# A gated delta-rule layer between two spline FFNs: two float16 halves with block scales instead of two float32r halves

## The reference

```python
qkvz = (x @ W_qkvz).reshape(b_, s_, NK, 2 * DK + 2 * R * DV)      # 16 heads of q, k; 32 of v, z; width 128
q, k, v, z = jnp.split(qkvz, [DK, 2 * DK, 2 * DK + R * DV], axis=-1)
ba = (x @ W_ba).reshape(b_, s_, NK, 2 * R)                          # beta and decay gates
# q, k, v: causal depthwise convolution of 4 taps, then silu; rms norm of q and k
def step(Sst, inp):
    q_t, k_t, v_t, g_t, beta_t = inp
    Sst = Sst * jnp.exp(g_t)[..., None, None]
    kv = jnp.einsum('bhk,bhkv->bhv', k_t, Sst)
    delta = (v_t - kv) * beta_t[..., None]
    Sst = Sst + k_t[..., None] * delta[:, :, None, :]
    o = jnp.einsum('bhk,bhkv->bhv', q_t, Sst)
    return (Sst, o)
# rms norm of o, times norm_w and silu(z), then @ W_out (4096 x 512), summed over the heads
```

## Time and profile before

| what | value |
|---|---|
| median of three runs | 3679.64 us |
| the profiled execution: span, first to last instruction | 3681.2 us |
| mean granted TensorE clock | 0.981 of 2.4 GHz |
| TensorE, matmuls | 3506.3 us busy, 95% |
| VectorE (DVE) | 2098.5 us, 57% |
| ScalarE (ACT) | 2087.1 us, 57% |
| GpSimd (POOL) | 2236.9 us, 61% |
| DMA | 268 MB moved, mean 73 GB/s |

### The profile page before, as it was taken

How to read it: one execution, slowest core, us unless ns; L and a number is a source line. 1 busy time by engine, 2 the same in 40 slices (tenths; PEclk the granted TensorE clock), 3 DMA queues, 4 the chain that set the end, 5 groups by cost and what they waited for, 6 DMA issues and landing times. The chain is left out here.

```text
span 3681.2 us, 77106 instructions
## 1 busy us (share of the span) xinstructions
PE 3506.3 (95%) x29092; PEld 2930.4 (80%) x29092; DVE 2098.5 (57%) x4063; ACT 2087.1 (57%) x5699; POOL 2236.9 (61%) x2675
## 2 busy tenths in 40 slices
PE   5997799999999999999999999999999999995998
PEld 3885588888888888888888888888888888884787
DVE  4654555555555555555555555555555555552564
ACT  3433566666666666666666666666666666662343
POOL 2112677777777777777777777777777777762110
PEclk8998899999999999999999999999999999997999
DMA  3415122222222221222222222222222122211421
GB/s 147 137 47 81 37 70 71 70 71 70 71 70 71 70 71 70 71 70 71 70 71 70 71 70 71 70 71 70 71 70 71 70 71 70 70 59 61 142 58 35
DMA packets 206383, 268.05 MB, mean 73 GB/s; under 512 B 86080, under 2 KB 116800, under 8 KB 204864
## 3 DMA queue, kind: packets, MB, share of 16 engines
q1 hardware_dynamic: 196752, 247.21, 20.5%
q0 software_dynamic: 4464, 14.36, 1.0%
q10 hardware_dynamic: 4800, 1.56, 0.3%
HBM read 173.76 MB, written 89.13 MB: 71 GB/s over the span
## 5 line engine op out<-in xcount | busy, mean ns | idle before, releaser
L1977 ACT ACTIVATE at_t<-at_inv 128x512 f16<-128x512 f32 x768 | 460.2, 599 | 472.2 <-PE at_inv L1785 472.1
L2164 DVE TENSOR_TENSOR at_pml<-at_prod,at_cst 128x256 f16<-128x256 f32 x768 | 322.7, 420 | 215.8 <-PE at_prod L1559 198.7
L1559 PE MATMUL at_proj<-x_hi,at_w_hi 128*128 128x512 f32 x1024 | 436.4, 426 | 2.7 <-PEq L1148 2.7
L1559 PE MATMUL at_proj<-x_hi,at_w_lo 128*128 128x512 f32 x1024 | 420.4, 411 | 0.0
L1559 PE MATMUL at_proj<-x_lo,at_w_hi 128*128 128x512 f32 x1024 | 415.1, 405 | 0.0
L2312 POOL TENSOR_TENSOR at_gt_lo<-at_cst,at_gates 128x512 fp32r<-128x512 f32 x256 | 261.8, 1044 | 249.6 <-PE at_misc L1559 249.6
L1559 PE MATMUL at_proj<-at_w_lo,x_hi 128*128 128x256 f32 x1024 | 314.3, 307 | 0.0
L1559 PE MATMUL at_proj<-at_w_hi,x_hi 128*128 128x256 f32 x1024 | 309.5, 302 | 0.8 <-DVE at_cv_q L2087 0.8
L1783 PEld LDWEIGHTS at_inv<-at_pml,at_t 128*128 128x128 f16 x3072 | 207.0, 97 | 120.1 <-issue 86.9
L2087 DVE SCALAR_TENSOR_TENSOR at_cv_v<-at_proj,at_cw,at_cv_v 128x511 f32<-128x511 f32 (+2 forms) x384 | 287.5, 749 | 21.8 <-ACT at_cv_v L1901 8.3
L1559 PE MATMUL at_proj<-at_w_hi,x_lo 128*128 128x256 f32 x1024 | 298.5, 292 | 0.0
(11 more groups left out here) (293 smaller groups left out, 10638.7 us busy)
## 6 DMA issues: line engine op xcount, KB each, us to landing
rows<-x SPq DMA_DIRECT2D x64, 1024.0 KB, 5.6
x<-rows SPq DMA_DIRECT2D x64, 1024.0 KB, 4.2
at_gb<-decays SPq DMA_DIRECT2D x64, 512.0 KB, 3.6
at_raw<-w_qkvz SPq DMA_DIRECT2D x45, 512.0 KB, 3.6
ffn_weights<-ffn_w SPq DMA_DIRECT2D x1, 11776.0 KB, 36.7
ffn_w<-ffn_weights POOLq DMA_DIRECT2D x4, 2688.0 KB, 23.8
at_raw<-w_out SPq DMA_DIRECT2D x16, 512.0 KB, 3.5
f_xnext<-x_in SPq DMA_DIRECT2D x4, 1024.0 KB, 5.1
```

What stands on the lines that cost most here:

```text
L1559: return nc.tensor.matmul(out, lhsT, rhs, start=start, stop=stop)
L1977: own["a_t"].up(A(grown(t16[:, s % R].rearrange("p a t -> p (a t)"), s // R), grown(psT[s % R], s // R), ACT.Copy))
L2164: own["d_p"].up(V.tensor_tensor(pml[:, level - 1, g].rearrange("p (c b a m) -> p c b a m", c=CH, a=2, m=m)[:, :, :, 0, :], psP[:, 0:S // 2 ...
```

## The change

All large operands become float16 instead of float32r, still high and low: `x_hi`, `x_lo`, `w_hi`, `w_lo`, `wo_hi`, `wo_lo`, `gt_hi`, `gt_lo`, `ba_hi`, `ba_lo`. To keep them in float16's range, x is scaled by 2^11 (in the layer norm's factor), and each block of weights (k and q, v, z, output, gates) by a power of two from its largest element, which is found on the chip: DVE reduces the raw weights along each partition, SP stores the 128 x 4 maxima to DRAM and loads them back into all partitions, DVE reduces again, keeps the exponent bits and makes a table `tab` of scales and inverse scales. POOL multiplies the raw weights by the scale before it splits them. The inverse scales go into the convolution taps (`cw`), ACT's tanh of z, and the add of the output product. norm_w leaves the gated output's copy and goes into the output weights.

The raw weights get buffers of their own (`raw_w` for three parts, `raw_o`), so that SP loads all of the next head pair's in the first unit; `gm` gets memory of its own and `mask_g(0)` and `low` lose their waits. In the norm phase the gate weights are scaled and split at chunk 7 instead of 3, and POOL's split of the first head pair's weights stands behind the scales, which DVE makes among the gates.

```diff
+def power_of_two(V, chain, mp, spread, mask, n):
+    chain(V.tensor_reduce(mp[:, 0:n], spread[:, :, 0:n].rearrange("p q n -> p n q"), mybir.AxisListType.X, ALU.max, apply_absolute_value=True))
+    chain(V.tensor_scalar(mp[:, 0:n], mp[:, 0:n], TINY, None, ALU.max))
+    chain(V.tensor_tensor(mp[:, 0:n].bitcast(I32), mp[:, 0:n].bitcast(I32), mask[:, 0:n], ALU.bitwise_and))
+
+def head_scales(V, chain, tab, mp, rcp, factors):
+    chain(V.reciprocal(rcp[:], mp[:]))
+    V.tensor_tensor(tab[:, 0:4], rcp[:], factors[:, 0:4], ALU.mult)
+    chain(V.tensor_tensor(tab[:, 4:8], mp[:], factors[:, 4:8], ALU.mult))
+    return V.tensor_tensor(tab[:, 7:8], tab[:, 7:8], mp[:, 2:3], ALU.mult)
...
@@ norm_phase, POOL @@
                     if c == 3:
-                        pool.wait_ge(consts_in, 64)
+                        pool.wait_ge(small_in, 32)
+                        nc.gpsimd.tensor_scalar(factors[:, 3:4], nw[:], 2.0 ** W_EXP, None, ALU.mult).then_inc(factors_set, 1)
+                    if c == 7:
+                        pool.wait_ge(ba_scaled, 1)
+                        nc.gpsimd.tensor_scalar(w_ba[:], w_ba[:], ba_tab[:, 0:1], None, ALU.mult).then_inc(split, 1)
...
+                pool.wait_ge(head_scaled, 1)
                 for i in range(3):
                     at = slice(i * PART, (i + 1) * PART)
-                    pool.wait_ge(raw_in[i], 16)
-                    nc.gpsimd.tensor_copy(w_hi[:, :, at], raws[i][:]).then_inc(w_split, 1)
+                    nc.gpsimd.tensor_scalar(raw_w[:, i], raw_w[:, i], tab[:, 0, i:i + 1], None, ALU.mult).then_inc(w_split, 1)
...
@@ norm_phase, DVE @@
                 for c in range(NCH - 3, NCH):
                     low(c)
+                    dve.wait_ge(raw_in[c - NCH + 3], 16)
+                    nc.vector.tensor_reduce(most[:, c - NCH + 3:c - NCH + 4], raw_w[:, c - NCH + 3].rearrange("p j n -> p (j n)"),
+                                            mybir.AxisListType.X, ALU.max, apply_absolute_value=True).then_inc(head_max, 1)
...
+                    if i == 0:
+                        dve.wait_ge(head_back, 16)
+                        dve.wait_ge(factors_set, 2)
+                        power_of_two(nc.vector, chain, mp, spread, exponent, 4)
+                        head_scales(nc.vector, chain, tab[:, 0, :], mp, rcp, factors).then_inc(head_scaled, 1)
...
@@ attn_phase, SP @@
                 if kh + 1 < NK:
+                    if kh > 0:
+                        sp.wait_ge(sems["p_w"], 2 * kh)
+                        sp.wait_ge(sems["p_z"], kh)
+                    load_part(sp, kh + 1, 0, "l_kq")
+                    load_part(sp, kh + 1, 1, "l_v")
+                    load_part(sp, kh + 1, 2, "l_z")
                     sp.wait_ge(sems["p_wo"], R * (kh + 1))
-                    load_part(sp, kh + 1, 0, "l_kq", raw_w)
+                    sp.dma_start(raw_o[:], w_out[(kh + 1) * (R * D):(kh + 2) * (R * D), :].rearrange("(r p) n -> p r n", p=P)).then_inc(sems["l_wo"], 16)
                 load_decays(first + 2)
                 next_rows(first + 1)
+                if kh + 1 < NK:
+                    sp.wait_ge(sems["d_max"], 4 * (kh + 1))
+                    sp.dma_start(most_dram, most[:]).then_inc(most_stored, 16)
+                    sp.wait_ge(most_stored, 16 * (kh + 1))
+                    sp.dma_start(spread[:].rearrange("p q n -> p (q n)"), most_dram.rearrange("q n -> (q n)").partition_broadcast(P)).then_inc(sems["l_most"], 16)
                 load_decays(first + 3)
...
@@ attn_phase, ACT @@
-                    own["a_thz"].up(A(th[:, u % 2, :], unit_bank[u][:], ACT.Tanh, scale=0.5))
+                    own["a_thz"].up(A(th[:, u % 2, :], unit_bank[u][:], ACT.Tanh, scale=tab[:, kh % 2, 6:7]))
...
-                    own["a_gt"].up(A(gt_hi[:, h, :], out_bank[:], ACT.Copy, scale=nw[:, 0:1]))
+                    own["a_gt"].up(A(gt_hi[:, h, :], out_bank[:], ACT.Copy, scale=2.0 ** GATED_EXP))
...
@@ attn_phase, DVE @@
-                    wait(dve, "s_dg", R * j if has_prep else R * (j - 1))
-                    own["d_lo"].up(V.scalar_tensor_tensor(gt_lo[:, h, :], out_bank[:], nw[:, 0:1], gt_hi[:, h, :], ALU.mult, ALU.subtract))
+                    own["d_lo"].up(V.scalar_tensor_tensor(gt_lo[:, h, :], out_bank[:], 2.0 ** GATED_EXP, gt_hi[:, h, :], ALU.mult, ALU.subtract))
...
-                    own["d_y"].up(V.tensor_tensor(row, out_bank[:], row, ALU.add))
+                    own["d_y"].up(V.scalar_tensor_tensor(row, out_bank[:], tab[:, of // B % 2, 7:8], row, ALU.mult, ALU.add))
+
+                def largest(i):
+                    new = j // B + 1
+                    wait(dve, ("l_kq", "l_v", "l_z", "l_wo")[i], 16 * (new + 1))
+                    if i < 3:
+                        own["d_max"].up(V.tensor_reduce(most[:, i:i + 1], raw_w[:, i].rearrange("p j n -> p (j n)"), mybir.AxisListType.X, ALU.max,
+                                                        apply_absolute_value=True))
+                    else:
...
+                if has_delta and j // B + 1 < NK:
+                    if j % B == 1:
+                        for i, s in enumerate((4, 9, 10, 13)):
+                            steps[s].append(lambda i=i: largest(i))
+                    if j % B == 2:
+                        steps[4].append(next_scales)
...
@@ attn_phase, POOL @@
+                wait(pool, "d_tab", kh + 1)
...
                     if hbs[0] == 0:
-                        G.tensor_copy(cw[kh % 2][:, 2 * part:2 * part + 2, :], cw_raw[:, 2 * part:2 * part + 2, :])
+                        G.tensor_scalar(cw[kh % 2][:, 2 * part:2 * part + 2, :], cw_raw[:, 2 * part:2 * part + 2, :], tab[:, kh % 2, 4 + part:5 + part], None, ALU.mult)
...
-                chain(G.tensor_copy(w_hi[:, part_rows, at], raw_w[:, part_rows]))
-                ins = G.tensor_tensor(w_lo[:, part_rows, at], raw_w[:, part_rows], w_hi[:, part_rows, at], ALU.subtract)
+                raw = raw_w[:, part, part_rows]
+                chain(G.tensor_scalar(raw, raw, tab[:, kh % 2, part:part + 1], None, ALU.mult))
+                chain(G.tensor_copy(w_hi[:, part_rows, at], raw))
+                ins = G.tensor_tensor(w_lo[:, part_rows, at], raw, w_hi[:, part_rows, at], ALU.subtract)
...
+                chain(G.tensor_scalar(raw_o[:, h], raw_o[:, h], tab[:, kh % 2, 3:4], None, ALU.mult))
+                chain(G.tensor_copy(wo_hi[:, h], raw_o[:, h]))
+                own["p_wo"].up(G.tensor_tensor(wo_lo[:, h], raw_o[:, h], wo_hi[:, h], ALU.subtract))
...
-                    wait(pool, "s_w", WPROD * j)
                     mask_g(0)
```

More of the change, by code:

```diff
@@ L1118, in norm_phase @@
         expo = sb("expo", [P, NK, NCH, R])
-        raws = [sb(f"raw{i}", [P, HB, HEADCOL // 3]) for i in range(3)]
         turn = [ctx.enter_context(nc.psum_tensor(f"nm_turn{i}", [P, 512], F32)) for i in range(3)]
@@ L1249, in copy_ba_T @@
                         act.wait_ge(ba_done, b - 1)
-                    nc.scalar.activation(ba_T[:, b % 2, :], ba_T_ps[b % 2][0:2 * NV, :], ACT.Copy).then_inc(baT_copied, 1)
+                    nc.scalar.activation(ba_T[:, b % 2, :], ba_T_ps[b % 2][0:2 * NV, :], ACT.Copy,
+                                         scale=ba_tab[0:2 * NV, 1:2]).then_inc(baT_copied, 1)
                 def scale(c):
@@ L1308, in gates_of @@
                     if b == 0:
-                        pe.wait_ge(split, 2)
+                        pe.wait_ge(split, 3)
                     if b >= 2:
@@ L2131, in out_add, with next_scales @@
                     row = rows[of % 2][:, c, :]
-                    own["d_y"].up(V.tensor_tensor(row, out_bank[:], row, ALU.add))
+                    own["d_y"].up(V.scalar_tensor_tensor(row, out_bank[:], tab[:, of // B % 2, 7:8], row, ALU.mult, ALU.add))
[4 more added lines that the diff above has]
+                        own["d_max"].up(V.tensor_reduce(most[:, i:i + 1], raw_w[:, i].rearrange("p j n -> p (j n)"), mybir.AxisListType.X, ALU.max,
+                                                        apply_absolute_value=True))
+                    else:
+                        chain(V.tensor_reduce(most[:, 3:4], raw_o[:].rearrange("p r n -> p (r n)"), mybir.AxisListType.X, ALU.max,
+                                              apply_absolute_value=True))
+                        own["d_max"].up(V.tensor_scalar(most[:, 3:4], most[:, 3:4], nw[:, 0:1], None, ALU.mult))
+                def next_scales():
+                    new = j // B + 1
+                    wait(dve, "l_most", 16 * (new + 1))
+                    power_of_two(V, chain, mp, spread, exponent, 4)
+                    own["d_tab"].up(head_scales(V, chain, tab[:, new % 2, :], mp, rcp, factors))
                 steps = {s: [] for s in range(STEPS)}
@@ L2382, in _ @@
                         sp.sem_clear(sems[n])
-                for one in spent[1::2] + [pml_set, out_done]:
+                for one in spent[1::2] + [pml_set, out_done, most_stored]:
                     sp.sem_clear(one)
@@ L2494 @@
```

(3 more changed lines are left out.)

139 lines of the change are left out of this document (86 added, 53 removed).

## The result

| | us |
|---|---|
| before, median of four runs beside the runs of after | 3678.2 |
| after, median of four runs (3830.7 to 3836.6) | 3831.4 |
| ratio, 95% interval | 1.0422 [1.0407, 1.0437] |
| forecast | 3682 (3635 to 3735) |
| profiled execution, span: before, after | 3681.2, 3830.2 |

What follows compares the result with a forecast made beforehand. The prediction took PE (TensorE) to lead, with POOL's and DVE's chains setting some pieces of each unit. 3681.2 - 90 + 86 + 7 - 1 = 3683.2 us for the span, so 3682 us for the median; range 3635 to 3735.

Steps and rivals of the forecast that it cites:

- POOL, multiplying raw weights in place: Scaling before POOL's split in the attention phase: 1.1 us for 1024 columns, 0.64 for 512; upper end 2.4 and 1.28.
- piece A: From a unit's last read-out (s_o) to turn_gated(0): POOL's 5.8 us chain sets it, half precision gains 0.
- second rival: POOL pays the two-input price for its multiplications: 4.5 us a head pair, +68, 3750 us; chance 0.15.
- Half precision, -90: Float16 matmuls in the repeated units: 0.216 us per 512-column step, -1.42 us a unit, times 63.
- rival 4: Float16 doesn't stream faster than float32r on PE: +41, 3723 us; chance 0.03.
- E: Residual and Newton with eight V matmuls on PE, until turn_kn: -0.31 us a unit.
- F: Recurrence with 24 projection matmuls in its gaps before s_o: -0.35 us a unit.
- A to D: Unit's pieces from s_o through the output products to steps 11 to 13: 0, -0.30, -0.41 and -0.05 us.
- next_scales, 2.85: DVE's table making in the third unit's fourth step, held off by POOL's instructions: 2.85 us, 0.43 without that rule.
- Rival 1: The lock doesn't hold for operations on four elements: 36 us less, 3646 us; chance 0.20.
- Norm phase, +7: DRAM round trips, reductions and POOL's later splitting before the units: +7 us, half of a 0 to 13 range.
- Rival 3: PE's new waits, above all in the third unit, let its clock fall to 1.2 GHz: +30, 3712 us; chance 0.10.

Runs made afterwards that it cites:

- e12: e3 with constants in the norm phase's tables, gate weights split at chunk 3, head weights split ahead of the gates, no reductions, trips or multiplications there; 3603.2 us.
- e1: The kernel after, without POOL's multiplications of the raw weights in the attention phase; 3689.8 us, ratio 1.0040.
- e3: The kernel after, without scale finding and without weight multiplications in the attention phase; 3624.4 us, ratio 0.9859.
- e2: The kernel after, without scale finding in the attention phase, the first head pair's table used for all; 3768.4 us, ratio 1.0251.
- e8: The kernel after, with next_scales in the second unit's recurrence, reductions behind the Newton step, loads ahead of rows, ACT multiplying, also in the norm phase; 3635.5 us.
- e11: e8 with next_scales ahead of minus_l and, in the norm phase, gate maxima through PE instead of DRAM and gate weights split at chunk 4; 3625.0 us.

## Why the prediction was wrong

The account, in profiled spans, against the terms of the forecast:

| term | forecast | measured | from |
|---|---|---|---|
| float16 operands | -90, -1 | -79 | e12 - before |
| reductions and next_scales | 15 x 3.5 = +52 | +65 | e1 - e3 |
| POOL's multiplications | 15 x 2.2 + 0.75 = +34 | +145 | e2 - e3 |
| norm phase | +7 | +20 | e3 - e12 |
| the two losses overlap | | -2 | |
| sum | +2 | +149 | |

The first row holds all of the change that e12_plain keeps, the buffers and the order of the loads too; by medians it is -76. The overlap can't be told from nothing. The losses of the second and third row include what the clock's falls cost.

**The step that failed** is "POOL, multiplying raw weights in place ... I take 1.1 and 0.64, for the select is the nearest operation". It costs 2.85 and 1.57, above even "upper: two inputs, 1.28 for 512 and 2.4 for 1024". No row had this opcode on such a tile, and the term was taken from the nearest other one. With the measured prices the forecast's own arithmetic gives the lateness that the trace shows. Output weights: two multiplications 3.14 - 0.22 - (0.67 - 0.28) = 2.53, read 2.58. Part 1: 2.85 - 0.24 - (1.06 - 0.28) = 1.83, read 4.58 - 2.51 = 2.07; part 2 read 1.79. Before `rr`: 1.15 + 1.57 - 0.64 = 2.08, read 9.70 - 8.02 = 1.68 (start of the last output matmul to that of turn_kn in the third unit, e2_no_scales against e3_halves_only; the other units have 7.84, so 0.18 of the 1.9 of e1's expectation is there without any multiplication). The recorded 1.15 itself doesn't follow from its terms as written: 0.70 + 0.77 - 0.25 is 1.22. Together 8.12 a head pair, 15 times that and the first head pair's output weights (2.6) 124 us; the remaining 21 of the 145 fit the 28 clock falls of e2_no_scales at 0.7 to 1.1 us. The mechanism (POOL's slack at the unit's end, piece A beginning with POOL) was right, and so was the second rival's; its price of 3750 us took the two-input price as the ceiling. The range was too narrow for this reason alone: both ends of the term came from other opcodes, and with 34 us in place of 145 and everything else as measured the span would be 3719 us, inside it.

The Trainium skill says that one-input operations of GpSimd run at about line rate (GPSIMD Engine Reference, Engine selection). The trace agrees for CAST (1.04 us for 1024 columns, where DVE's reduction of as many takes 1.21) and disagrees for TENSOR_SCALAR, which takes 2.7 times CAST's time; the measurement decides.

**Half precision, -90.** The step of 0.216 was right (0.215), which refutes rival 4, and so was its place. A plain unit takes 44.60 us, 1.27 less and not 1.42. E gave 0.19 instead of 0.31 (turn_kn now starts 0.12 us behind the end of ACT's scaled k, before 0.32) and F 0.28 instead of 0.35; A to D gave what they should (0.80, forecast 0.76). The 63 units make 74 us less in e12_plain, and 6 more come at the ends.

**next_scales, 2.85**, was right: turn_gated(1) comes 2.65 us later in the third unit. The detail was off, and it is partly luck that the size came out: the reduction takes 1.08 us and not 0.6, and the operation held first is the maximum with a constant, which has one input and was taken as free, not the bit mask behind it. Not in the forecast were the clock's fall behind that wait (0.8 to 1.2 us more before the first output product, in 12 of the 15 units) and 1.1 us instead of **0.65** for the four reductions. Rival 1, no lock on four elements, is refuted by the 0.95 and 0.90 us.

**Norm phase, +7.** It measured +20, above the range of 0 to 13, which left out the trip through DRAM, called "partly hidden": 7.75 us of idle DVE and 11.4 us of delay for PE (the step from chunk 3 to chunk 7 included), and 9.6 us of POOL's split alone at the end. Which of the two makes how much of the 20 us isn't separated; e8 and e11 took back 4 and 3 us by one each.

**The clock.** Rival 3 was given as a case of its own (3712 us), with 2 us for each fall on one place per head pair. The mechanism was right, place and price weren't: the falls came along with the other costs, behind many of the late unit starts too, at 0.7 to 1.1 us each.

**What would show it.** Right: the steps of 0.215, the third unit longest, DVE operations of about 1 us, no idle time before `at_dcy`. Wrong: POOL's 0.6 and 1.1, the third unit longer than a plain one by 4 (it is 51.31 against 44.60, 6.7), and the norm phase's growth of more than 15 us, which had been named as what would refute the forecast.

**A version that beats both.** e11_best computes all that after computes and runs at 0.9844 of before, 3625 us: the scales cost it 24 us over e12_plain instead of 228.

## What to carry to other kernels

Price an operation by its own opcode: on POOL the same product by a per-partition factor costs 1.57 us as TENSOR_SCALAR and 1.04 as TENSOR_TENSOR with a broadcast operand, and where no row has the opcode, the range has to reach past the nearest ones. Read how long the engine whose chain starts the next unit is idle before it (POOL here: 0.7 to 1.1 us behind a split): what new work takes beyond that is lost for every engine, so put it into another engine's gap first (ACT here). In this kernel a wait of TensorE of 2 us or more cost 0.7 to 1.1 us more where its clock fell behind it.
